# A two-layer graph network on one core: one tile in place of two at a layer's end, edge rows loaded in two pieces, output through a padded table

## What is computed

```python
xn  = layernorm(x, ln1)
xp  = xn + xn @ Wpos + bpos + deg * Wdeg + bdeg      # deg: normalised out-degree
q, k, v = xp @ Wq + bq, xp @ Wk + bk, xp @ Wv + bv   # 8 heads of 16
att = clip(sum(q[dst] * k[src]) / 4, -50, 50)        # per edge and head
x   = x + (segment_softmax(att, dst) @ v[src]) @ Wo + bo
x   = x + gelu(layernorm(x, ln2) @ W1 + b1) @ W2 + b2    # hidden width 512
```

## Time and profile before

| | us |
|---|---|
| median of 3 runs | 2145.94 |
| lowest, highest | 2145.27, 2147.04 |
| the profiled execution, its own time | 2146.24 |
| its span, first to last instruction | 2144.0 |

### The profile page before, as it was taken

How to read it: one execution, slowest core, us unless ns; L and a number is a source line. 1 busy time by engine, 2 the same in 40 slices (tenths; PEclk the granted TensorE clock), 3 DMA queues, 4 the chain that set the end, 5 groups by cost and what they waited for, 6 DMA issues and landing times.

```text
span 2144.0 us, 44177 instructions
## 1 busy us (share of the span) xinstructions
PE 1429.2 (67%) x11694; PEld 1269.1 (59%) x11695; DVE 1457.1 (68%) x2503; ACT 920.0 (43%) x1639; POOL 1489.5 (69%) x1584
## 2 busy tenths in 40 slices
PE   2757656766777777776554666676677677777555
PEld 2547655655666666665543665565566566666554
DVE  4987766656777677676557666666677767777654
ACT  1334433334555555554225333332455555555323
POOL 0067777777777777777736777777777777777773
PEclk9868897788999889788677888777889988888767
DMA  2145555455555555555524554554455555555541
GB/s 63 39 160 174 164 164 154 155 162 155 160 171 161 159 166 165 158 165 169 160 59 158 159 160 154 160 158 153 155 163 163 161 162 158 159 166 157 168 150 52
DMA packets 120419, 321.60 MB, mean 150 GB/s; under 512 B 31428, under 2 KB 43834, under 8 KB 120320
## 3 DMA queue, kind: packets, MB, share of 16 engines
q0 software_dynamic: 75072, 205.10, 31.8%
q1 hardware_dynamic: 44410, 113.69, 16.1%
q10 hardware_dynamic: 838, 1.60, 0.3%
HBM read 311.92 MB, written 8.35 MB: 149 GB/s over the span
## 4 chain that ended last, share of the span: by engine, by line
POOL 64%; issue 22%; DVE 5%; PE 4%; DMA 1%; SPq 1%; DVEq 1%; ACT 1%; ACTq 0%; POOLq 0%
POOL kv L560 64%; DVE q_parts L837 1%; PE ps L1342 1%; DMA kv<-kv_tab,src_idx 1%; SPq L440 1%; DMA kv<-in_dst 1%; DVE msg L1104 1%; DVE qkv L924 0%; DVE dots L1080 0%; PE ps L1304 0%; SPq L441 0%; PE ps L1298 0%; PE ps L1195 0%; DVEq L356 0%; DVE prod L1070 0%
## 5 line engine op out<-in xcount | busy, mean ns | idle before, releaser
L560 POOL DMA_INDIRECT kv<-kv_tab,src_idx x1564 | 1485.7, 950 | 622.6 <-issue 474.6
L1342 PE MATMUL ps<-msg,hot 128*128 128x136 f32 x3896 | 665.3, 338 | 370.7 <-DVE acc L985 363.6
L1342 PEld LDWEIGHTS ps<-msg,hot 128*128 128x128 f32 x3896 | 613.1, 239 | 414.3 <-DVE msg L1104 237.8
L1327 PE MATMUL ps<-q_parts,hotT 128*128 x5844 | 467.5, 242 | 221.4 <-DVE prod L1070 171.3
L1327 PEld LDWEIGHTS ps<-q_parts,hotT 128*128 x5844 | 415.7, 109 | 286.0 <-issue 265.4
L1070 DVE TENSOR_TENSOR prod<-kv,ps 128x1024 f32<-128x1024 f32 (+1 forms) x198 | 238.4, 1204 | 267.6 <-DMA kv<-kv_tab,src_idx 244.1
L990 DVE SCALAR_TENSOR_TENSOR hot<-dst_col,neg_base,ps 128x1024 f32<-128x1024 f32 (+1 forms) x246 | 311.8, 1267 | 125.0 <-issue 117.2
L696 ACT ACTIVATE dist<-dst_rows,neg_node 128x1024 bf16<-128x1024 int32 x246 | 282.5, 1148 | 140.9 <-issue 126.3
L705 ACT ACTIVATE msg<-att 128x64 f32<-128x64 f32 (+1 forms) x198 | 49.9, 252 | 595.6 <-DVE att L1085 594.9
L699 ACT ACTIVATE hotT<-dist 128x1024 bf16 x246 | 259.9, 1057 | 50.1 <-ACT dist L696 44.4
L1080 DVE TENSOR_REDUCE dots<-prod 128x64 f32<-128x1024 f32 (+1 forms) x198 | 238.8, 1206 | 28.9 <-DVE prod L1070 23.9
(11 more groups left out here) (221 smaller groups left out, 972.6 us busy)
## 6 DMA issues: line engine op xcount, KB each, us to landing
dst_rows<-in_dst SPq DMA_DIRECT2D x194, 512.0 KB, 4.1
kv<-kv_tab,src_idx POOLq DMA_INDIRECT x1564
kv_tab<-qkv SPq DMA_DIRECT2D x26, 128.0 KB
kv_tab<-qkv SPq DMA_DIRECT2D x3, 768.0 KB, 3.8
out<-z SPq DMA_DIRECT2D x24, 64.0 KB
hot<-in_L_gnn_W SPq DMA_DIRECT2D x2, 256.0 KB
w<-in_L_gnn_W SPq DMA_DIRECT2D x2, 256.0 KB
kv_tab<-qkv SPq DMA_DIRECT2D x1, 512.0 KB, 3.8
```

The lines of the kernel that those rows point to most:

```text
L560: pool.indirect_dma_start(kv[:, u, c, :], None, kv_tab[l][:, :], bass.IndirectOffsetOnAxis(ap=src_idx[:, c, at(g)], axis=0)).then_inc(kv_i ...
L1327: last = MM(qd[:, c * P:(c + 1) * P], hotT[:, bass.ds(pr % 2, 1), c * P:(c + 1) * P], q_parts[:, at(t), k * D:(k + 1) * D], start=first an ...
L1342: last = MM(agg, hot[:, u % 2, c, :], msg[:, u % 2, c, :], start=(c == 0), stop=(c == nch - 1))
```

## The change

- The 97 whole edge rows are loaded as 96 rows (partitions 3 to 98) and one row (partition 2), for `src` and `dst` each. ACT waits for eight loads in place of six.
- `TAIL` is 1 and the slots take tiles from 24 downwards, so all of tiles 24 to 1 may go into slots. Only tile 0 is left for the end.
- At the end, the output projection's bias row goes first, before the wait for `agT`; `z1T` is copied by DVE and not by ACT; the hidden quarters lie in four PSUM banks, each with its own signal to the gelu, which signals each quarter to the second matmul (`h_part`, `hid_part`); that one's bias row goes first.
- In the last layer a slot's tile is stored to a new table `out_tab` in device memory, with 25 whole tiles. After the last broadcast SP copies rows 128 to 3124 of it to the output in one DMA, device memory to device memory, and stores tile 0 straight to the output. It waits for both at the end.

```diff
@@ constants and layout @@
-TAIL_TILES = (NT - 1, 0)
-TAIL = len(TAIL_TILES)
+TAIL = 1
...
-        hid = [hid_slot[:, :]] + [kv_flat[:, u * FF:(u + 1) * FF] for u in range(1, TAIL)]
+        hid = [hid_slot[:, :]]
...
-        in_tail = [{"agT": bank(2 * f, P), "o": bank(2 * f + 1, P), "z1T": bank(2 * f, P),
-                    "h": [ps[:, 2 * f + 1, c * P:(c + 1) * P] for c in range(FC)],
-                    "y": bank(2 * f, P), "z2T": bank(2 * f + 1, P), "qkv": bank(2 * f, 3 * D)} for f in range(TAIL)]
+        in_tail = {"agT": bank(0, P), "o": bank(1, P), "z1T": bank(7, P), "h": [bank(2 + c, P) for c in range(FC)],
+                   "y": bank(6, P), "z2T": bank(0, P), "qkv": bank(1, 3 * D)}
...
+        out_tab = nc.dram_tensor("out_tab", [NT * P, D], F32)
@@ SP @@
             for rows, d in ((src_i, src_d), (dst_i, dst_d)):
-                sp.dma_start(rows[2:NG, :], d[FIRST + SECOND:E].rearrange("(g e) -> g e", e=GE)).then_inc(edges_in, 16)
+                sp.dma_start(rows[3:NG, :], d[FIRST + SECOND + GE:E].rearrange("(g e) -> g e", e=GE)).then_inc(edges_in, 16)
             sp.wait_ge(rows_clear, 2)
             for rows, d in ((src_i, src_d), (dst_i, dst_d)):
+                sp.dma_start(rows[2:3, :], d[FIRST + SECOND:FIRST + SECOND + GE].rearrange("(g e) -> g e", g=1)).then_inc(edges_in, 16)
                 sp.dma_start(rows[1:2, 0:SECOND], d[FIRST:FIRST + SECOND].rearrange("(g e) -> g e", g=1)).then_inc(edges_in, 16)
...
-                        to = out_d[t * P:t * P + rows, :] if isinstance(t, int) else out_d[bass.ds(t * P, P), :]
-                        sp.dma_start(to, z2[s][0:rows, :]).then_inc(row_out[l], 16)
+                        to = out_d[t * P:(t + 1) * P, :] if isinstance(t, int) else out_tab[bass.ds(t * P, P), :]
+                        sp.dma_start(to, z2[s]).then_inc(row_out[l], 16)
...
                 stored(n)
-                for f, t in enumerate(TAIL_TILES):
-                    ready(n + f + 1)
-                    store(t, f, N - t * P if t == NT - 1 else P)
+                if l == L - 1:
+                    sp.dma_start(out_d[P:N, :], out_tab[P:N, :]).then_inc(out_copied, 16)
+                ready(n + 1)
+                store(0, 0)
                 if l == L - 1:
                     stored(n + TAIL)
+                    sp.wait_ge(out_copied, 16)
@@ ACT @@
-            act.wait_ge(edges_in, 96)
+            act.wait_ge(edges_in, 128)
...
+                copy_agT(n, 0, in_tail)
+                scale_x2(n, 0)
                 gelu_only()
-                for f in range(TAIL):
-                    copy_z1T(n + f, f, in_tail[f])
-                for f in range(TAIL):
-                    gelu(n + f, f, in_tail[f])
+                for c in range(FC):
+                    act.wait_ge(h_part[l], c + 1)
+                    nc.scalar.activation(hid[0][:, c * P:(c + 1) * P], in_tail["h"][c], ACT.Gelu, bias=b1f[:, l, c:c + 1]).then_inc(hid_part[l], 1)
                 log_and_exp()
@@ DVE: in slot_words_out, slot_tile and early_tile NT - 2 becomes NT - 1; at the end @@
+                share_out(0, n, 0)
+                add_attention(0, n, 0, in_tail, x2[0])
+                normalise_x2(n, 0, x2[0])
+                dve.wait_ge(z1T_ps[l], n + 1)
+                nc.vector.tensor_copy(z1T[0], in_tail["z1T"]).then_inc(z1T_done[l], 1)
+                add_ffn(0, n, 0, in_tail, x2[0])
+                normalise_x3(0, n, 0)
+                next_row(0, n, 0, in_tail)
@@ PE @@
-                for part in (transpose_ag, project_out, transpose_z1, hidden, project_ffn, transpose_z2, project_next):
-                    for f in range(TAIL):
-                        part(n + f, f, in_tail[f])
+                transpose_ag(n, 0, in_tail)
+                MM(in_tail["o"], ones[0:1, :], bo_row[:, l, :], start=True, stop=False)
+                pe.wait_ge(agT_done[l], n + 1)
+                MM(in_tail["o"], agT[0], wo[:, l, :], start=False, stop=True).then_inc(o_ps[l], 1)
+                transpose_z1(n, 0, in_tail)
+                pe.wait_ge(z1T_done[l], n + 1)
+                for c in range(FC):
+                    MM(in_tail["h"][c], w1g[:, l, c * P:(c + 1) * P], z1T[0], start=True, stop=True).then_inc(h_part[l], 1)
+                MM(in_tail["y"], ones[0:1, :], b2_row[:, l, :], start=True, stop=False)
+                for c in range(FC):
+                    pe.wait_ge(hid_part[l], c + 1)
+                    last = MM(in_tail["y"], hid[0][:, c * P:(c + 1) * P], w2[:, l, c, :], start=False, stop=(c == FC - 1))
+                last.then_inc(y_ps[l], 1)
+                transpose_z2(n, 0, in_tail)
+                project_next(n, 0, in_tail)
```

More of the change, by code:

```diff
@@ L210, in gnn_program @@
         hid_slot = sb("hid_slot", [P, FF])
[L211 to L214, removed]
+        ag, agT, x2, x3, z1T, z2, z2T = ([one[:, :]] for one in one_of_each.values())
+        z1 = [z[:, 0, :]]
         x2_of = [x2[0], x2_odd[:, :]]
-        hid = [hid_slot[:, :]] + [kv_flat[:, u * FF:(u + 1) * FF] for u in range(1, TAIL)]
+        hid = [hid_slot[:, :]]
         ps = ctx.enter_context(nc.psum_tensor("ps", [P, 8, 512], F32))
@@ L342, in gnn_program @@
         numbers_read = sem("numbers_read")
+        h_part = sems("h_part")
+        hid_part = sems("hid_part")
+        out_copied = sem("out_copied")
         block = ctx.enter_context(nc.Block())
@@ L388, in slot_tile @@
         def slot_tile(eng, j):
-            t = eng.value_load(slot_tab[0:1, bass.ds(j, 1)], min_val=0, max_val=NT - 2)
-            return eng.snap(t.with_bounds(min_val=0, max_val=NT - 2))
+            t = eng.value_load(slot_tab[0:1, bass.ds(j, 1)], min_val=0, max_val=NT - 1)
+            return eng.snap(t.with_bounds(min_val=0, max_val=NT - 1))
         def tail_start(eng):
@@ L415, in early_tile @@
         def early_tile(eng, done):
[L417 removed]
+            return eng.snap((NT - 1 - done).with_bounds(min_val=0, max_val=NT - 1))
         def tail_number(eng):
@@ L467, in _, with store @@
             for l in range(L):
-                def store(t, s, rows=P):
+                def store(t, s):
                     if l < L - 1:
@@ L768, in _ @@
                 n = tail_number(act)
-                for f in range(TAIL):
-                    copy_agT(n + f, f, in_tail[f])
-                for f in range(TAIL):
-                    scale_x2(n + f, f)
+                copy_agT(n, 0, in_tail)
+                scale_x2(n, 0)
                 gelu_only()
-                for f in range(TAIL):
-                    copy_z1T(n + f, f, in_tail[f])
-                for f in range(TAIL):
-                    gelu(n + f, f, in_tail[f])
+                for c in range(FC):
+                    act.wait_ge(h_part[l], c + 1)
+                    nc.scalar.activation(hid[0][:, c * P:(c + 1) * P], in_tail["h"][c], ACT.Gelu, bias=b1f[:, l, c:c + 1]).then_inc(hid_part[l], 1)
                 log_and_exp()
-                for f in range(TAIL):
-                    scale_x3(n + f, f)
-                for f in range(TAIL):
-                    copy_z2T(n + f, f, in_tail[f])
+                scale_x3(n, 0)
+                copy_z2T(n, 0, in_tail)
         @block.vector
@@ L1158, in _ @@
                         next_row(t, m, 0, in_slot)
-                tail = [(t, n + f, f) for f, t in enumerate(TAIL_TILES)]
-                for t, m, f in tail:
-                    share_out(t, m, f)
-                for t, m, f in tail:
-                    add_attention(t, m, f, in_tail[f], x2[f])
-                for t, m, f in tail:
-                    normalise_x2(m, f, x2[f])
-                for t, m, f in tail:
-                    add_ffn(t, m, f, in_tail[f], x2[f])
-                for t, m, f in tail:
-                    normalise_x3(t, m, f, before=n)
-                for t, m, f in tail:
-                    next_row(t, m, f, in_tail[f], before=n)
+                share_out(0, n, 0)
[6 more added lines that the diff above has]
+                next_row(0, n, 0, in_tail)
                 if l < L - 1:
```

6 lines of the change are left out of this document (3 added, 3 removed).

## The result

Beside the kernel before on the same chip (median 2145.99 us of 4 runs) the changed kernel took **2107.18 us**, the median of 4 runs from 2105.46 to 2108.54: a ratio of 0.9819, 95% interval 0.9807 to 0.9832, 38.8 us less. The prediction was 2107.8 us. The difference is 1.8% of the time, and the interval lies clear of 1. Two more measurements of the same kernel gave 2112.15 against 2148.53 and 2110.36 against 2148.98, so 36.4 and 38.6 us less. The profiled execution took 2108.54 us, its span is 2106.6.

What follows compares the result with a forecast made beforehand. POOL's two gather streams bound the kernel, so only start, layer gap and end could shrink: 28.8 + 4.3 + 5.0 = 38.1 us off 2146.24 gives 2108.1, median 0.3 lower, 2107.8 us. Range 2102 to 2116, 8 in 10.

Steps and rivals of the forecast that it cites:

- The statistics need x by 14.7: Start: DVE's statistics need x by 14.7 us; all 2.9 MB at 264 GB/s should be there by 12.5.
- a sign of being wrong: Start: the prediction called itself wrong if DVE waits for x over 2 us.
- the forecast's best bound: Start: at best DVE doesn't wait at all, its block 6 starts at 25.0, 30.3 us gained.
- Rival (a): Start: x or the weights come late and bound it; price 4 us, 2111.8 us; chance 0.12.
- without the bias behind it, the sum starts 0.72 us sooner: First layer's end: with the bias no longer behind the projection, its sum starts 0.72 us sooner, at 1113.36.
- the bias (0.72): Layer's end: PE's bias product between hidden's 8 instructions and the second product's 8, taken as 0.72 us.
- the train of 4.5 us: Layer's end: PE's hidden, bias and second product in a row, 1.8 + 0.7 + 1.8 + 0.2 = 4.5 us.
- PE's slow pace: First layer's end: the 384-column pair takes 1.32 us as at the start, not 0.81; 0.51 us lost.
- only a prime count of rows is seen on one: Output copy: taken as spread over several engines, since only a prime row count was seen on one; 0 us cost.
- The nine engines of the other reading: Output copy: by the Trainium skill's rule 2997 rows go on nine engines, 6.6 us, with the sum the same.
- (b): Output copy: runs on one engine at 26 GB/s, lands at 2128.5, total 2130.4 us; chance 0.08.
- (c): Output copy: one engine at half the rate, 13 GB/s, lands at 2178.4, total 2180.3 us; chance 0.03.

Runs made afterwards that it cites:

- experiment 1: The kernel before with only its edge rows loaded as 96 and 1; 2118.14 us, ratio 0.9858.
- experiment 8: Kernel of Experiment 7 plus bf16 filler products on zeros in the tail, two before the transpose of ag, three before that of z1; 2110.63 us, ratio 0.9822.
- experiment 6: Changed kernel, table rows 1 KB apart with 512 B used, copied as 2971 rows (a prime) and 26; 2145.17 us, ratio 0.9976.
- Experiment 9: Changed kernel, weights issued only after x landed, square root before the wait for the second half of the row transposes; 2110.74 us, ratio 0.9825.
- experiment 2: Changed kernel with tile 0 alone in the tail, but worked in the old order of steps; 2112.72 us, ratio 0.9838.
- Experiment 7: Changed kernel with both bias products of the tail one step earlier, ahead of the transposes of ag and z1; 2107.79 us, ratio 0.9816.
- experiment 5: Changed kernel, table rows 1 KB apart with 512 B used, 2997 rows in one copy; 2110.09 us, ratio 0.9818.
- experiment 3: Changed kernel without the copy and its wait, output rows 128 to 3124 unwritten; 2108.89 us, ratio 0.9816.

## Why the prediction was right, and where it wasn't

**The start: right, by its own steps.** PE's transposes "start at 16.1": 15.90. "block 6 starts at 26.4": 26.30. "POOL starts at 86.3": 86.77. The loads moved at 246 GB/s instead of 264, the rows were there at 12.3 (13.2 said), and experiment 1 shows that the split alone does it. "The statistics need x by 14.7", with "the thinnest margin": x came later, and DVE waited 1.60 us for it. It cost next to nothing here: ACT finished the square root at 25.52 and DVE its block 5 at 25.73, so both chains met at the reciprocal. But the wait differs from execution to execution. Eleven profiled executions have this same start. In seven of them the wait is 0.3 to 0.8 us, and block 6 starts at 26.1 to 26.2. In two of the changed kernel it is 1.60 and 1.76, block 6 at 26.30 and 26.34. In experiments 8 and 6 it is 2.30 and 2.55, over the 2 us that the prediction had set as a sign of being wrong, and block 6 starts at 26.89 and 27.15. Experiment 9 shortened both and gained the 1.5 us that the forecast's best bound (block 6 at 25.0) had named. Rival (a), another transfer as the bound, was thus half met, by the transfer that it had named, x's 53 rows, and at 0.2 us here and up to 1 us in others instead of 4. A split of those rows wasn't tried.

**The slots: right.** No tile early, no tile late. The reading of the earlier trace rows behind it was loose: its 200 quarters are those of 23 useful slots, the useless one and tile 24 at the end, and tile 0's 8 stand apart.

**The ends: the mechanism right, three terms mis-sized and one not constant.** The sum with x was put 9.6 us after share_out and came at 10.21. "without the bias behind it, the sum starts 0.72 us sooner": the order was right, but ahead of the projection the bias pair starts only at 1083.18, so the projection waits for it until 1083.91, and 0.44 us is what is gained (2.54 us from share_out to the sum, 2.98 in experiment 2's kind of end). Experiment 7 shows that it can't be had back by moving the bias further. "the bias (0.72)" inside the train of 4.5 us took 1.02; the train was 4.84, and without the bias, in experiment 7, 3.82, which is just what the other terms of the 4.5 make. The 384-column pair took 1.65 us, where I had 1.32 from the start for PE's slow pace. That row was a mixture: in the kernel before the clock is granted at 1.00 from 57 to 58 us and at 0.52 on average from 58 to 60. Here it was the slow level for all of the pair. These are 0.3 + 0.3 + 0.3 of the 0.9 us missing at the first end. At the last end the pair isn't there; 0.6 are the same two terms, and from tile 0's store to the end of the span it took 2.98 us instead of 2.08, which was held constant. So 1.4 us (5.0 - 3.6) are missing there. The cause of that last 0.9 stays open, but the kept traces narrow it. It is 2.98, 3.14 and 3.12 us in the three executions of the changed kernel, and there one of the store's 16 end writes comes 0.6 to 0.8 us after the others. It is 2.03 in experiment 2's and 2.22 in experiment 5's, which have a copy too, so the copy alone doesn't bring it.

**The copy: right in the sum, for a reason that wasn't the real one.** Issued at 2060.55 (2058.4 said), landed 8.3 us later, one product late and caught up, no time lost (experiment 3). But "only a prime count of rows is seen on one" drew the wrong line: a prime count is spread too when its rows lie end to end. The nine engines of the other reading weren't it either: 16 end writes. Rivals (b) and (c) were not a matter of 2997 = 27 x 111, as there was no such danger here at all. Where it was real, in experiment 6, the price of (b) was too low: 2145 us, not 2130.4. The copy was issued at 2065.0 and not at 2058.4, which is 6.6 us, and the last 1.16 MB of it moved at 21.8 GB/s after the gathers had ended, where 26 was taken, which is another 8.7. That puts the landing of the rival's own terms (2080 + 1.21 MB / 26 GB/s = 2126.5) at 2141.8, and it was 2142.4. The prediction says 2128.5 there and 2178.4 in (c): both sums are 2 us above what their terms give, without a word on it. That SP is held behind such a copy, which its 14.19 us in the issue of a 2 KB row had shown in the trace before, was left out of the rival too, but it moved the end by 0.2 us at most.

**That it came so near is in part luck.** For the profiled execution the errors cancel: 0.4 us at the start and 2.3 at the ends were forecast too much, 1.5 came from the drains and 0.7 from the streams unasked, and 0.7 in all (with rounding) are left. The median then fell 0.6 us on the other side of the forecast, as the profiled execution was the slowest of the four. What drains and streams gave isn't shown to be the change's: the other two profiled executions of the changed kernel had a second drain of 12.43 and 11.98 us (12.49 before), and first streams of 980.79 and 983.30.

## What to carry to other kernels

Look in the windows for a DMA share of one engine in sixteen: here it was each time a transfer whose row count has no divisor up to 16 and whose rows don't lie end to end (97 and 2971), and splitting off one row was worth 28 us, against 7 for the whole work on the two ends. The queue that issued such a transfer was held as well, so count what is queued behind it. When a serial end is reordered, an instruction put ahead of the critical one is free only if its engine is idle there for its whole length.

## What the runs showed of the hardware

- Rows that lie end to end in device memory on both sides were copied spread, at both numbers tried: 2997 rows in 8.3 us, 2971 (1.52 MB) in 6.8 us, each in 32 equal packets with 16 end writes. With a gap between the rows, 2997 went in 12.8 us with nine end writes, and 2971 on one engine at 22 GB/s with one.
- While such a transfer ran, the issuing engine's next DMA was held: 14.19 us behind the edge loads, 73.81 us behind the copy. It isn't only transfers on one engine: ACT's issue of x's last rows was held 7.31 us behind the spread load of the other 24 tiles.
- PE's granted clock stayed at 0.50 with PE busy for 6.6 of 7 us (experiment 8), and averaged 0.89 from 1090 to 1092 in experiment 7's kernel, where PE was busy for 3.22 of the 4 us before. What raises it is left open.
- The stream of the same 782 gathers took from 980.8 to 985.1 us in the first layer and from 979.1 to 981.3 in the second, in different executions. So gains of 2 to 3 us in this kernel show only in the pieces of a profile.
